# Cross attention with a gate: scores as extra columns of the gate's matmuls, softmax tile by tile, V's gate part in a PSUM bank of its own

## The reference

```
qp = x @ Wq + bq;  kp = ctx @ Wk + bk;  vp = ctx @ Wv + bv
w = softmax(qp @ kp.T / sqrt(D))
a = w @ vp
gate = concat(qp, a) @ Wg + bg
out = a * mask * sigmoid(gate) + x
```

## Time and profile before

| | |
|---|---|
| median of 3 runs | 416.56 us (416.47 to 417.1) |
| time of the profiled execution | 416.89 us |
| its span, first to last instruction | 415.1 us |
| busy: PE, DVE, ACT, POOL | 407.6, 228.9, 144.7, 124.0 us |
| weight loads (PEld) | 325.5 us, 1874 of them |

### The profile page before, as it was taken

How to read it: one execution, slowest core, us unless ns; L and a number is a source line. 1 busy time by engine, 2 the same in 40 slices (tenths; PEclk the granted TensorE clock), 3 DMA queues, 4 the chain that set the end, 5 groups by cost and what they waited for, 6 DMA issues and landing times.

```text
span 415.1 us, 5234 instructions
## 1 busy us (share of the span) xinstructions
PE 407.6 (98%) x1874; PEld 325.5 (78%) x1874; DVE 228.9 (55%) x404; ACT 144.7 (35%) x251; POOL 124.0 (30%) x96
## 2 busy tenths in 40 slices
PE   8999999999999999999999999999999999999995
PEld 4889986888776878787787878778787877878784
DVE  3687557554563646547364554736455564645554
ACT  5644242325223414233241414424241432324121
POOL 0005125445635405052340505133150504325000
PEclk9999999999999999999999999999999999999999
DMA  7993542568699795866859576786958677595412
GB/s 267 384 415 130 148 130 109 203 200 292 206 305 269 255 304 171 253 196 226 261 189 286 191 252 204 230 221 214 280 199 263 190 242 225 205 275 199 132 53 101
DMA packets 42934, 92.11 MB, mean 222 GB/s; under 512 B 4780, under 2 KB 4780, under 8 KB 42268
## 3 DMA queue, kind: packets, MB, share of 16 engines
q1 hardware_dynamic: 41756, 89.68, 66.4%
q10 hardware_dynamic: 1152, 2.10, 1.6%
HBM read 64.75 MB, written 27.00 MB: 221 GB/s over the span
## 4 chain that ended last, share of the span: by engine, by line
PE 93%; POOL 2%; ACT 2%; DMA 1%; DVE 1%; issue 0%; DVEq 0%
PE bank L430 42%; PE bank L323 32%; PE bank L454 3%; PE bank L461 3%; PE bank L460 3%; PE bank L453 3%; PE bank L346 3%; PE bank L442 2%; POOL xT L781 1%; PE bank L401 1%; DMA wkT_raw<-in_wkT 1%; PE bank L383 1%; POOL wg L781 1%; ACT vT L488 0%; ACT wg L484 0%
## 5 line engine op out<-in xcount | busy, mean ns | idle before, releaser
L430 PE MATMUL bank<-wqg,xT 128*128 128x512 f32 x768 | 192.4, 396 | 0.0
L430 PEld LDWEIGHTS bank<-wqg,xT 128*128 128x128 f32 x768 | 142.1, 188 | 30.6
L781 POOL TENSOR_TENSOR xT<-x_raw,xT 128x512 fp32r<-128x512 f32 x64 | 87.5, 1397 | 178.7 <-ACT xT L493 178.7
L744 DVE SCALAR_TENSOR_TENSOR prod_sb<-tanh_sb,bank 128x512 f32<-128x512 f32 x64 | 43.9, 686 | 72.2 <-ACT tanh_sb L587 72.2
L587 ACT ACTIVATE tanh_sb<-bank 128x512 f32<-128x512 f32 x64 | 38.3, 598 | 125.0 <-PE bank L454 124.3
L755 DVE SCALAR_TENSOR_TENSOR out_sb<-prod_sb,half_mask,x_rows 128x512 f32<-128x512 f32 x64 | 54.5, 851 | 1.7
L323 PE MATMUL bank<-xT,mt 128*77 128x512 f32 x192 | 47.1, 394 | 0.8 <-POOL xT L781 0.8
L323 PEld LDWEIGHTS bank<-xT,mt 128*77 128x77 f32 x192 | 27.8, 146 | 16.9 <-POOL xT L781 1.3
L493 ACT ACTIVATE xT<-x_raw 128x512 fp32r<-128x512 f32 x64 | 35.3, 622 | 0.4 <-DMA x_raw<-in_xT 0.4
L323 PE MATMUL bank<-wv,ctxT 128*128 128x512 f32 (+1 forms) x120 | 30.2, 401 | 0.0
L323 PE MATMUL bank<-wg,vT 128*128 128x512 f32 (+1 forms) x120 | 29.7, 394 | 0.4 <-DVE vT L612 0.3
(11 more groups left out here) (73 smaller groups left out, 354.2 us busy)
## 6 DMA issues: line engine op xcount, KB each, us to landing
x_rows<-in_x SPq DMA_DIRECT2D x32, 512.0 KB, 6.9
out_y<-out_sb SPq DMA_DIRECT2D x64, 256.0 KB, 4.3
x_raw<-in_xT SPq DMA_DIRECT2D x60, 256.0 KB, 10.4
v_ext<-v_dram SPq DMA_DIRECT2D x32, 308.0 KB
v_dram<-v_st SPq DMA_DIRECT2D x18, 512.0 KB, 3.3
v_ext<-v_dram SPq DMA_DIRECT2D x16, 180.0 KB
ctxT_raw<-in_ctxT SPq DMA_DIRECT2D x4, 624.0 KB, 10.6
ctx_rows<-in_ctx SPq DMA_DIRECT2D x4, 616.0 KB
```

What stands on the lines that cost most here:

```text
L430: pe.matmul(gate_ps[n % 3][:, :], xT[b % 2][:, s, c, q], wqg[:, m, c, :], start=(c == 0 and (s, m) == PRODUCTS[0]), stop=False)
L744: dve.scalar_tensor_tensor(prod_sb[:, n % 2, :], tanh_sb[:, n % 2, :], 1.0, attn_ps[n % 2][:, :], ALU.add, ALU.mult).then_inc(prod_made, 1)
L781: pool.tensor_tensor(dst, src, f32(hi_), ALU.subtract).then_inc(made, 1)
```

## The change

`wqg` goes into a buffer `ws` beside the batch's columns of `mt`. One row chunk of it is two halves of HN = 296 columns each: 39 columns of scores, one empty, 256 of the gate. `main(n)` makes gate and scores of tile n in 24 matmuls of 296 columns into a pair of banks, with xT stationary, where `gate_main` had 12 of 512 columns and `scores_T` 12 per batch. `scores_T`, `add_sb` and `turn_scores` are gone; the softmax comes out with rows on partitions and is done per tile, with the bias from a row `sb_row` that is spread over the partitions by way of DRAM. V's gate part goes to a bank of its own; ACT copies the gate from the main pair into `gx` (`x_part`), DVE adds V's part (`gate`), ACT takes tanh of that. There are two `ws` buffers; POOL places the batch's `mt` columns (`place_mt`). ACT splits one chunk of the next batch's xT per tile.

```diff
+HK = SP // 2
+HN = HK + 1 + D // 2
...
+        main_ps, vgate_ps, attn_ps, turn_ps = [psum[:, 4:6], psum[:, 0:2]], bank[2:4], bank[6], bank[7]
...
+            def main(n, chunks):
+                b, q = n // T, slice(n % T * P, (n % T + 1) * P)
+                ps = main_ps[n % 2]
+                if chunks[0] == 0:
+                    pe.wait_ge(xT_lo, (b + 1) * C)
+                    pe.wait_ge(mt_placed, b + 1)
...
+                    else:
+                        pe.wait_ge(gx_made, n - 1)
+                for c in chunks:
+                    for s, m in PRODUCTS:
+                        for h in range(2):
+                            last = pe.matmul(ps[:, h, 0:HN], xT[b % 2][:, s, c, q], ws[b % 2][:, m, c, h, :],
+                                             start=(c == 0 and (s, m) == PRODUCTS[0]), stop=(c == C - 1 and (s, m) == PRODUCTS[2]))
+                if chunks[-1] == C - 1:
+                    last.then_inc(main_done, 1)
...
+            for n in range(NT + 2):
+                if 0 < n < NT:
+                    main(n, range(0, C // 2))
+                if n >= 2:
+                    attend(n - 2)
+                if n < NT:
+                    main(n, range(C // 2, C - 1))
+                if 1 <= n <= NT:
+                    turn_probs(n - 1)
+                if n < NT:
+                    main(n, range(C - 1, C))
```

```diff
+            def x_part(n):
+                act.wait_ge(main_done, n + 1)
+                act.wait_ge(sc_made, n + 1)
...
+                act.activation(gx[:, n % 3, :].rearrange("p (h n) -> p h n", h=2), main_ps[n % 2][:, :, HK + 1:HN], ACT.Copy).then_inc(gx_made, 1)
...
+            for n in range(1, NT + 2):
+                if n <= NT:
+                    x_part(n - 1)
+                    exps(n - 1)
+                b, c = (n - 1) // T + 1, (n - 1) % T
+                if b < B:
+                    act.wait_ge(main_done, (b - 1) * T)
+                    act.wait_ge(xT_in[c], 16 * (b + 1))
+                    act.activation(xT[b % 2][:, HI, c], x_raw[:, c], ACT.Copy).then_inc(xT_hi, 1)
+                if n >= 2:
+                    tanh_tile(n - 2)
+                if n <= NT:
+                    high_probs(n - 1)
```

```diff
+            def softmax_max(n):
...
+                dve.tensor_tensor(sc[:, i, :, :], main_ps[i][:, :, 0:HK], sb_row[:, :, :, b], ALU.add).then_inc(sc_made, 1)
...
+                dve.tensor_reduce(rowmax[:, t], sc[:, i, :, :].rearrange("p h k -> p (h k)"), AX.X, ALU.max).then_inc(max_made, 1)
...
+                dve.tensor_scalar(negmax[:, t], rowmax[:, t], -SCALE, None, ALU.mult).then_inc(negmax_made, 1)
...
+            for n in range(1, NT + 2):
+                if n <= NT:
+                    softmax_max(n - 1)
+                    softmax_rest(n - 1)
+                if n >= 2:
+                    gate(n - 2)
+                if n <= NT:
+                    low_probs(n - 1)
+                if n >= 2:
+                    product(n - 2)
+                    output(n - 2)
```

More of the change, by code:

```diff
@@ L71 @@
 C0 = B0 + 4096
-D0 = C0 + 4096
+D0 = C0 + 2 * 2 * C * HN
 E0 = D0 + 2 * C * KEYS
@@ L408, in _ @@
                 else:
-                    scores_T(0)
+                    main(0, range(0, C // 2))
                 n = KROWS[k - 1]
@@ L433, in turn_probs @@
-            def turn_probs(b):
-                pe.wait_ge(prob_made, b + 1)
-                pe.wait_ge(prob_twice, 2 * (b + 1))
-                if b == 0:
-                    pe.wait_ge(job_drained, last_in_bank(7))
-                else:
-                    pe.wait_ge(wTb_made, b)
-                    pe.wait_ge(wT_lo, b)
-                for t in range(T):
-                    last = pe.transpose(turn_ps[:, t * P:(t + 1) * P], prob[:, t, :], ident[:, :])
-                last.then_inc(turned, 1)
@@ L734, in low_probs @@
-            def low_probs(b):
-                dve.wait_ge(wTa_made, b + 1)
-                dve.tensor_tensor(wT[0:S, 1, :], turn_ps[0:S, :], f32(wT[0:S, 0, :]), ALU.subtract).then_inc(wT_lo, 1)
-            def product(b, t):
-                n = b * T + t
+                    dve.memset(sb_c[:, :], OUT_OF_SIGHT).then_inc(sb_filled, 1)
+                    dve.wait_ge(sb_filled, 1)
+                    dve.tensor_scalar(sb_c[0:S, :], sb_dot[:, :], bqbk[0:S, 0:1], None, ALU.add).then_inc(sb_made, 1)
@@ new lines, in low_probs, with gate, product @@
+            def low_probs(n):
+                q = slice(n % T * P, (n % T + 1) * P)
+                dve.wait_ge(wT_hi, n + 1)
+                dve.tensor_tensor(wT[0:S, 1, q], turn_ps[0:S, q], f32(wT[0:S, 0, q]), ALU.subtract).then_inc(wT_lo, 1)
+            def gate(n):
+                dve.wait_ge(vgate_done, n + 1)
+                dve.wait_ge(gx_made, n + 1)
+                dve.tensor_tensor(gx[:, n % 3, :], vgate_ps[n % 2][:, :], gx[:, n % 3, :], ALU.add).then_inc(pre_made, 1)
+            def product(n):
@@ L806, in _ @@
                     v_lo_of(k)
+                if k == 3:
+                    pool.wait_ge(job_drained, J["mt", MB * C - 1] + 1)
+                    pool.wait_ge(ws_cleared, 1)
+                    place_mt(0)
                 if k in (7, 8):
@@ L812, in _ @@
                     lo(v_st[(k - 1) % 2][0:n, LO, D:2 * D], vg_f[0:n, :], v_st[(k - 1) % 2][0:n, HI, D:2 * D], vg_lo)
+            pool.wait_ge(job_done, NJ)
+            pool.memset(f32(ws[1][:, :, :, :, 0:HK + 1]), 0.0).then_inc(ws_cleared, 1)
+            for s in range(2):
+                pool.tensor_copy(ws[1][:, s, :, :, HK + 1:HN], ws[0][:, s, :, :, HK + 1:HN]).then_inc(ws_copied, 1)
+            pool.wait_ge(ws_cleared, 2)
+            pool.wait_ge(ws_copied, 2)
+            place_mt(1)
             for b in range(1, B):
                 xT_lo_of(b)
+                if b + 1 < B:
+                    place_mt(b + 1)
 def kernel(**inputs):
```

264 lines of the change are left out of this document (108 added, 156 removed).

## The result

The changed kernel takes 570.13 us, the median of 4 runs (568.66 to 570.97), beside 416.82 for the kernel before on the same chip: a ratio of 1.3675, interval 1.3639 to 1.3711. The profiled execution took 568.66 us, 1.8 over its span of 566.9. The forecast was 520 (495 to 552). The kernel got slower for the reasons that were given, but by 50 us more than forecast, and 18 us beyond the top of the range.

A forecast was written before the change was run, and what follows sets the result against it. PE bound the kernel before; afterwards a DVE-ACT loop would. 127.3 + 64 x 4.95 + 15 x 3.80, with first-tile, last-tile and end corrections, gave 506.4; 15 for clock falls made about 521, stated as 520 (495 to 552).

The forecast's parts named there:

- PE's work: PE's matmuls, attend and transpose: 296-column matmuls 0.14 us apart, 4.40 us per tile, 17.6 per batch instead of 18.32.
- the rival of the weight loads: PE's main matmuls: weight loads of 188 ns follow one another without overlap, about 550 us; chance 0.08.
- The loop between DVE and ACT: Each tile's chain through DVE and ACT, addition to next addition: 4.95 us, bounds 4.8 and 5.3.
- The sum's 0.08: ACT's exp now also sums its row: 0.08 us added to its duration, bounds 0 and 0.28.
- The boundary: Between batches, xT's fourth chunk is split late and PE waits: 3.80 us more per boundary, 15 times.
- The clock: PE's clock falls after its rest at half of the 15 boundaries, 2.0 us each: 15 us.
- The row of the end of the span: Trace row of PE's rest at the program's end: the clock fell there after 4.1 us; boundary rest put at 5.2.
- The sum by that rule, 536: Forecast total if PE's clock falls at all 15 boundaries, by the Trainium skill's rule on rests: 536 us.
- The start: Before the first tile, the bias row loads behind the folding's last store: first addition at 127.3 us.
- Late x_raw: Rival: at xT's split ACT waits 3.7 us for x_raw's DMA, 14 times: +39, about 555 us; chance 0.10.
- Absorbed boundary: Rival: the batch boundary costs nothing extra, the loop of 4.95 us stays: 449 us; chance 0.06.
- PE as the bound: Rival: DVE and ACT's loop comes under 4.40 us, xT is in time, PE sets the pace: 411 us; chance 0.02.

The follow-up runs named there:

- Experiment 9: Changed kernel with output in the wait for exp, xT split earlier, exp before x_part, high_probs before tanh, bias stored early, x_raw loaded whole: 419.65 us.
- experiment 4: Changed kernel with exp's row sum left out, a constant in its place: 565.71 us, ratio 1.3582.
- experiment 2: Changed kernel with 32 unused matmuls of 296 columns on PE ahead of its wait for xT at each boundary: 533.58 us, ratio 1.2820.
- experiment 1: Changed kernel with xT's last two chunks both split in the batch's third tile, a tile ahead: 487.82 us, ratio 1.1726.
- Experiment 5: Changed kernel with the bias row's store and load ahead of the first V loads in SP's queue: 564.42 us, ratio 1.3563.
- experiment 8: Changed kernel with output, exp, high_probs and bias moved earlier, one xT chunk split per tile a tile ahead, x_raw loaded chunk by chunk: 464.62 us, ratio 1.1147.
- experiment 3: Changed kernel with exp ahead of x_part on ACT: 560.90 us, ratio 1.3474.
- experiment 6: On top of experiment 1, ACT makes wT's high part before tanh and its copy after: 468.94 us, ratio 1.1265.

## Where the prediction was right, and which of its terms failed

The mechanism was right: a loop of DVE and ACT longer than PE's work, a late chunk of xT at each boundary, and a clock that falls there. Three terms of the sum were too small: the clock (15 us taken, 36 measured), the loop (some 20 us short) and the start (4.7 short).

- **PE's work**: right. 296 columns were 0.136 us apart (6 matmuls in 0.98, one of them 0.30), 0.14 predicted. Experiment 9 shows the batch of 17.5 us, 17.6 predicted. Loads of 188 ns don't bind: the rival of the weight loads fell, and with it the rule of the Trainium skill ("TensorE: Matmul & The Clock Gate", section "The mechanism" in its Part 3) by which load and stream would add up.
- **The loop between DVE and ACT**: the mechanism and the place of each wait were right, the size was 4.95 for 5.26, inside the bounds given. The term that failed is small instructions. An overlap of 0.09 was taken for exp behind x_part, and there was a gap of 0.03. exp's duration was drawn on the line through 512 and 308 columns to 78, which gave 0.28 for 0.36. The three multiplications did overlap, but were taken too short: 0.35 for 0.46. The sum's 0.08 was right (experiment 4: 0.09). The 0.31 make 20 us in 64 tiles.
- **The boundary**: right. 3.80 predicted, 3.84 measured (experiment 2; experiment 1 shows that it goes when xT is early).
- **The clock**: the term that failed most. The mechanism was named, but only half of the boundaries were counted, at 2.0. All 15 fell, at 2.4 (experiment 2), so the term was 36 and not 15. The row of the end of the span was read as a threshold near the rest in question; it is one instance, and shows only that a rest of 4.1 had not yet brought the clock down there. By the Trainium skill ("TensorE: Matmul & The Clock Gate", section "Why this matters for your kernels") all fall, and the trace agrees: 15 of 15. The sum by that rule, 536, was nearer, and still 34 us short.
- **The start**: 127.3 predicted, 132.0 measured. SP's last store of the folding was issued 0.7 later than predicted; the step left out is the landing of the bias's own store, which the load waits for: 5.2 us more. Experiment 5 shows that it is on the path, worth 5.7 of the 9.2 us by which the addition came earlier.
- **The range**: its top of 552 took the loop at 5.2. With the loop at the 5.3 that the prediction itself gave as a bound, and all falls at 2.0, the sum is 506 + 22 + 30 = 559. With the measured sizes it is 506.4 + 64 x 0.31 + 15 x 2.40 + 4.7 = 567; the profiled execution took 568.66.
- **Late x_raw**: didn't happen in the changed kernel (4.9 us to landing in the median, 10.4 before). The reason given was that its loads have no V loads ahead of them. That isn't shown to be the whole of it: in experiment 9, with the loads at the same place in SP's queue, the median was 7.1, at a DMA share of 80% of a batch and not some 50%. The rival did come in experiment 8, which shortened the lead. Its price was added up wrongly: 39 on 521 is 560, not 555.
- **Absorbed boundary, PE as the bound**: fell. The point named for the second, a loop under 4.40, was reached only after the loop had been rearranged: in experiment 8 tiles of 4.0 came behind the stalls, and in experiment 9 PE's work set the pace, with tiles of mostly 4.3. That kernel came to 419.65, not the 411 of the rival: the start costs 9.5 us and not 6, and of the 10.8 that PE's work gains, 4.6 are lost at the end.

## What to carry to other kernels

An engine's saved work counts only at the pace of the slowest loop through all engines: write out one iteration start to start, with 0.15 us for each narrow DVE multiplication as measured here, not with a line drawn from wide ones, and look for work of another tile to put into each wait. Here the output, moved into the wait for exp, gave 51 us, far more than the 11.5 that the matmuls were to save. A lead that is spread evenly over tiles must still end a tile before the consumer, and the transfer behind it needs its own lead. Here PE's rests of 5.2 us were paid twice, once as the rest and once as the half clock behind it, at each of the 15: count such a term at every one of them, and add the bounds of all terms up for the range.

## What the runs showed of the hardware

- PE's clock fell behind each of the 15 rests of 5.2 us and stayed at 1.2 GHz for 6.8 us; it had fallen before PE resumed. In experiment 3, behind rests of 5.4 us, it was still low for 2.9 to 6.2 us when PE was back, and the boundary took 10.6 to 12.1 us accordingly. With fillers in the rest it never fell between the start and the end, and that kernel was 36.6 us faster. In experiment 1 it fell for 3.4 us behind a rest of 1.2 us in 6 of 15 batches, and behind the same rest in experiment 6, with shorter rests in the other tiles, in none. In experiment 8 it fell behind 5 of 11 rests of 1.6 to 3.1 us.
- exp with a sum is followed by a read of the accumulator of 187 ns in the mean, of which 90 lie on the path. exp started 0.03 after the end of the copy ahead of it.
- DVE's output of 512 columns took 1.19 us instead of 0.75 beside POOL's place_mt of 0.70, 14 times in experiment 1. In experiment 5 three narrow multiplications took 2.40 us instead of 0.55 beside POOL's copy of ws.
- After a store of 4.9 KB it took 10 us until the load behind it could go, from ACT's queue 7.3 at a DMA share of 99%, and 4.0 with V's loads held behind it and a share of 73%. In the first case its packets didn't start until 4.4 us after the issue, and the last one ran 9.6 us after it.
